# Layer 3 of a decoder kernel: the chosen half of the tokens gathered into 512 slots by one-hot products, and another order of subtractions and maxima in the image attention

## The reference, cut to what matters

```python
scores = (relu(x @ modr_w1 + modr_b1) @ modr_w2 + modr_b2)[..., 0] / TEMP
topk_scores, topk_idx = top_k(scores, k)           # k = 128 of 256
w = softmax(topk_scores, -1)
sorted_idx = sort(topk_idx, -1)
tok = take_along_axis(x, sorted_idx[..., None], axis=1).reshape(B_ * k, D_)
n1 = _ln(tok, ln1_w, ln1_b); uv = n1 @ m_in_w      # 128 -> 2 * 256
u = uv[:, :INNER] * m_conv_w[:, 3] + m_conv_b; res = uv[:, INNER:]
sp = u @ m_xproj_w                                 # 256 -> 33
y = u * (sp[:, 16:32].sum(-1) * sp[:, -1])[:, None] * silu(res)
tok = tok + y @ m_out_w
n2 = _ln(tok, ln2_w, ln2_b)
# gate: the two greatest of softmax(n2 @ moe_r_w + moe_r_b) over 8 experts, normalised
h1 = gelu(einsum('nd,edh->enh', n2, moe_w1) + moe_b1)   # hidden 512
tok = tok + gated sum over e of (h1 @ moe_w2 + moe_b2)
out = x.at[arange(B_)[:, None], sorted_idx].set(tok.reshape(B_, k, D_) * w[..., None])
```

## Time and profile before

| | before |
|---|---|
| runs, us | 4619.43, 4628.18, 4628.18 |
| profiled execution, its own time, us | 4625.78 |
| its span (first to last instruction), us | 4624.1 |
| PE busy | 3545.3 us, 77% |
| DVE busy | 3007.0 us, 65% |
| ACT busy | 1899.2 us, 41% |
| POOL busy | 390.9 us, 8% |
| mean granted TensorE clock | 0.868 |

### The profile page before, as it was taken

How to read it: one execution, slowest core, us unless ns; L and a number is a source line. 1 busy time by engine, 2 the same in 40 slices (tenths; PEclk the granted TensorE clock), 3 DMA queues, 4 the chain that set the end, 5 groups by cost and what they waited for, 6 DMA issues and landing times. The chain is left out here.

```text
span 4624.1 us, 53788 instructions
## 1 busy us (share of the span) xinstructions
PE 3545.3 (77%) x21514; PEld 1886.8 (41%) x21514; DVE 3007.0 (65%) x4129; ACT 1899.2 (41%) x2110; POOL 390.9 (8%) x150
## 2 busy tenths in 40 slices
PE   5699999999999955577777773556654776687569
PEld 3434444444444423233335552423322454454357
DVE  4466666666766676498896446599996455535541
ACT  2255555555555532244442223244442344344223
POOL 0001010100001000000000000044440000001000
PEclk9899999999999977799997896666667888798789
DMA  2000000000000000100002001000000110000000
GB/s 76 9 0 0 1 0 0 0 0 0 0 0 0 1 11 12 20 7 8 8 1 87 28 2 39 1 0 0 0 0 3 36 37 9 37 1 1 0 12 31
DMA packets 12876, 55.75 MB, mean 12 GB/s; under 512 B 2209, under 2 KB 2721, under 8 KB 11970
## 3 DMA queue, kind: packets, MB, share of 16 engines
q1 hardware_dynamic: 12626, 52.31, 3.8%
HBM read 48.50 MB, written 0.52 MB: 11 GB/s over the span
## 5 line engine op out<-in xcount | busy, mean ns | idle before, releaser
L985 PE MATMUL banks<-L0x_q_context,L0x_context 96*128 96x512 f32 (+1 forms) x1632 | 743.5, 597 | 10.8 <-ACT L0x_ring L1054 10.2
L996 PE MATMUL banks<-L0x_ring,L0x_context_rows 128*97 128x512 f32 (+1 forms) x1632 | 737.1, 594 | 1.8 <-ACT L0x_ring L1040 1.8
L1054 ACT COPY L0x_ring<-banks 128x1024 f32<-128x1024 f32 (+1 forms) x416 | 413.0, 995 | 648.4 <-PE banks L985 648.4
L1103 DVE TENSOR_TENSOR L0x_maxima<-L0x_maxima,L0x_ring 128x1024 f32<-128x1024 f32 (+1 forms) x288 | 342.7, 1195 | 261.1 <-ACT L0x_ring L1054 260.1
L1082 DVE TENSOR_TENSOR L0x_ring<-L0x_ring,L0x_greatest 128x2048 f32<-128x2048 f32 (+1 forms) x208 | 458.2, 2205 | 45.9 <-ACT L0x_ring L1054 45.9
L985 PEld LDWEIGHTS banks<-L0x_q_context,L0x_context 96*128 96x128 f32 (+1 forms) x1632 | 302.8, 188 | 415.2 <-issue 393.7
L996 PEld LDWEIGHTS banks<-L0x_ring,L0x_context_rows 128*97 128x97 f32 (+1 forms) x1632 | 263.7, 164 | 433.0 <-issue 429.7
L1040 ACT ACTIVATE L0x_ring<-L0x_ring 128x2048 f32<-128x2048 f32 (+1 forms) x208 | 384.1, 1847 | 8.6 <-DVE L0x_ring L1082 8.6
L1462 ACT ACTIVATE L1x_probs<-banks 128x2048 f32<-128x2048 f32 (+1 forms) x112 | 196.6, 1756 | 263.0 <-PE banks L1392 221.1
L1495 DVE TENSOR_REDUCE L1x_maxima<-banks 128x3 f32<-128x1203 f32 (+1 forms) x176 | 241.6, 1373 | 90.8 <-PE banks L1361 90.8
L1361 PE MATMUL banks<-L1x_k,L1x_q 32*128 32x401 f32 x1024 | 182.1, 593 | 119.7 <-DVE L1x_maxima L1495 104.3
(11 more groups left out here) (918 smaller groups left out, 5439.5 us busy)
## 6 DMA issues: line engine op xcount, KB each, us to landing
L1f_expert_weights<-in_L1f_experts SPq DMA_DIRECT2D x16, 512.0 KB, 9.6
L2f_expert_weights<-in_L2f_experts SPq DMA_DIRECT2D x8, 512.0 KB, 5.6
L3a_expert_weights<-in_L3a_experts SPq DMA_DIRECT2D x8, 512.0 KB, 4.9
L3f_expert_weights<-in_L3f_experts SPq DMA_DIRECT2D x8, 512.0 KB, 6.2
L1x_k<-L1x_k_rows SPq DMA_DIRECT2D x64, 50.0 KB
L0x_context_rows<-in_context_rows SPq DMA_DIRECT2D x1, 2448.0 KB, 29.1
L0x_context<-in_context SPq DMA_DIRECT2D x1, 2401.5 KB, 20.6
L1x_context<-in_context SPq DMA_DIRECT2D x4, 600.4 KB, 5.0
```

The source lines that it names most:

```text
L985: mm = pe.matmul(k.ps[0:height(j), i, :], c1[:, j * P:j * P + height(j)], q1[:, u // 2 % 2, :], start=True, stop=True)
L996: mm = pe.matmul(k.ps[0:CW, bank, :], rows1[0:height(j), j, :], ring[0:height(j), s % RING, i, :], start=s == FIRST[u] and i == 0, stop=s ...
L1054: act.copy(ring[0:r, s % RING, 2 * p:2 * p + len(pair), :], k.ps[0:r, 2 * p:2 * p + len(pair), :]).then_inc(copied, 1)
L1103: dve.tensor_tensor(o, before, ring[0:r, s % RING, 2 * p:2 * p + m, :], ALU.max).then_inc(maxed, 1)
```

## The change

`normalise_columns`, `linear_columns`, `linear_rows`, `one_hot`, `experts`, `gate_bias` and `softmax_experts` get a parameter `tiles` (8 where not given). In `layer3_attention` a chosen token's position plus one (0 for others) is compared with the numbers 1 to 128, which gives a one-hot matrix `into` for each tile. Products of `into` with the rows put the 512 chosen tokens into 4 tiles `picked`, and everything up to the experts runs with `tiles=4`. The transposed one-hots (`back`) put weighted result minus `picked` back to the tokens' places at the end, straight onto the residual; the unchosen rows come in by an addition in the slot stage, and the softmax weights are looked up by slot in one pass. In `attend_image` DVE's order becomes another.

```diff
 def experts(..., tiles=TILES):
+    halves = tiles // 4
...
-                first(0, 0)
-                first(0, 1)
+                for half in range(halves):
+                    first(0, half)
                 for e in range(E):
-                    for half in range(2):
+                    for half in range(halves):
                         second(e, half)
                         if e + 1 < E:
                             first(e + 1, half)
...
 def layer3_attention(k):
...
             @block.tensor
...
                 mm.then_inc(counted, 1)
+                for t in range(TILES):
+                    pe.wait_ge(spread, t + 1)
+                    mm = pe.matmul(k.ps[:, 1, t // TPB * P:(t // TPB + 1) * P], into[:, t, :], z0[:, t, :],
+                                   start=t % TPB == 0, stop=t % TPB == TPB - 1)
+                mm.then_inc(gathered, 1)
+                for t in range(TILES):
+                    mm = pe.transpose(k.ps[:, 2 + t // 4, (t % 4) * P:(t % 4 + 1) * P], into[:, t, :], k.ident[:])
+                mm.then_inc(turned, 1)
             @block.scalar
             def _(act):
+                act.wait_ge(gathered, 1)
+                act.copy(picked[:].rearrange("p b c -> p (b c)"), k.ps[:, 1, :])
                 act.wait_ge(ready, 1)
                 act.activation(sB[:], sB[:], ACT.Exp).then_inc(exped, 1)
+                act.wait_ge(turned, 1)
+                act.copy(back[:].rearrange("p t c -> p (t c)"), k.ps[:, 2:4, :].rearrange("p a n -> p (a n)"))
             @block.vector
...
+                dve.wait_ge(counted, 1)
+                step(dve.scalar_tensor_tensor(out=at[:], in0=k.ps[:, 0, 0:TILES], scalar=1.0, in1=chosen[:], op0=ALU.add, op1=ALU.mult))
+                for t in range(TILES):
+                    dve.tensor_scalar(into[:, t, :], k.count[:], at[:, t:t + 1], None, ALU.is_equal).then_inc(spread, 1)
                 step(dve.tensor_reduce(best[:, 0], s4, X, ALU.max))
                 dve.tensor_tensor(s4, s4, best[:, 0, :, None].broadcast_to(full), ALU.subtract).then_inc(ready, 1)
+                dve.tensor_tensor(k.x[:], k.x[:], z0[:], ALU.add)
                 dve.wait_ge(exped, 1)
                 step(dve.scalar_tensor_tensor(out=sB[:], in0=rB[:], scalar=CAP - 0.5, in1=sB[:], op0=ALU.is_lt, op1=ALU.mult))
                 step(dve.tensor_reduce(best[:, 0], s4, X, ALU.add))
-                step(dve.reciprocal(best[:, 1], best[:, 0]))
-                step(dve.tensor_tensor(s4, s4, best[:, 1, :, None].broadcast_to(full), ALU.mult))
-                dve.wait_ge(counted, 1)
-                step(dve.tensor_copy(at[:], k.ps[:, 0, 0:TILES]))
-                for t in range(TILES):
-                    step(dve.scalar_tensor_tensor(out=tmp[:, 0], in0=r4[:, t // TPB], scalar=at[:, t:t + 1], in1=s4[:, t // TPB],
-                                                  op0=ALU.is_equal, op1=ALU.mult))
-                    step(dve.tensor_reduce(weight[:, t:t + 1], tmp[:, 0], X, ALU.add))
-        normalise_columns(k, z0, k.z, k.zT, column_gain=w["gain"], column_shift=w["shift"])
+                dve.reciprocal(best[:, 1], best[:, 0])
+                step(dve.scalar_tensor_tensor(out=sB[:], in0=rB[:], scalar=slot[:], in1=sB[:], op0=ALU.is_equal, op1=ALU.mult))
+                step(dve.tensor_reduce(weight[:], s4, X, ALU.add))
+                step(dve.tensor_tensor(weight[:], weight[:], best[:, 1], ALU.mult))
+        normalise_columns(k, picked, k.z, k.zT, column_gain=w["gain"], column_shift=w["shift"], tiles=B)
...
-        experts(k, "L3a", ew, k.zT, gates, acc, w["mb1"], ACT.Gelu, ImageLast(k.image_ahead))
+        experts(k, "L3a", ew, k.zT, gates, acc, w["mb1"], ACT.Gelu, ImageLast(k.image_ahead), tiles=B)
...
+            @block.tensor
+            def _(pe):
+                for t in range(TILES):
+                    pe.wait_ge(changed, t // TPB + 1)
+                    pe.matmul(k.ps[:, t // 4, (t % 4) * P:(t % 4 + 1) * P], back[:, t, :], tok[:, t // TPB, :], start=True, stop=True).then_inc(returned, 1)
             @block.vector
             def _(dve):
-                step = Steps(dve, own)
-                full = [P, TILES, P]
-                step(dve.tensor_tensor(tok[:], tok[:], acc[:], ALU.add))
-                step(dve.tensor_tensor(tok[:], tok[:], weight[:, :, None].broadcast_to(full), ALU.mult))
-                step(dve.tensor_tensor(tok[:], tok[:], z0[:], ALU.subtract))
-                step(dve.tensor_tensor(tok[:], tok[:], chosen[:, :, None].broadcast_to(full), ALU.mult))
-                step(dve.tensor_tensor(tok[:], tok[:], z0[:], ALU.add))
-        accumulate(k, tok)
+                dve.tensor_tensor(tok[:], tok[:], acc[:], ALU.add).then_inc(added, 1)
+                dve.wait_ge(added, 1)
+                for b in range(B):
+                    dve.scalar_tensor_tensor(out=tok[:, b, :], in0=tok[:, b, :], scalar=weight[:, b:b + 1], in1=picked[:, b, :],
+                                             op0=ALU.mult, op1=ALU.subtract).then_inc(changed, 1)
+                for half in range(2):
+                    dve.wait_ge(returned, 4 * half + 4)
+                    x = k.x[:, 4 * half:4 * half + 4, :].rearrange("p t c -> p (t c)")
+                    dve.tensor_tensor(x, x, k.ps[:, half, :], ALU.add)
...
 def attend_image(...):
...
-            maximum(0)
+            first_half(0)
+            third(0)
+            fold(0)
+            first_half(1)
             for b in range(B):
+                shift(b, 0)
                 if b + 1 < B:
-                    maximum(b + 1)
-                shift(b)
+                    third(b + 1)
+                shift(b, 1)
+                shift(b, 2)
+                if b + 1 < B:
+                    fold(b + 1)
+                shift(b, 3)
                 if b >= 2:
                     finish(b - 2)
+                if b + 2 < B:
+                    first_half(b + 2)
```

More of the change, by code:

```diff
@@ L220, with normalise_columns @@
 ACT_TILES = (3, 6, 7)
-def normalise_columns(k, src, rows, dstT, gain=None, shift=None, column_gain=None, column_shift=None, eps=1e-5, values=None):
-    shared = ACT_TILES if gain is None else ()
-    mine = [t for t in range(TILES) if t not in shared]
+def normalise_columns(k, src, rows, dstT, gain=None, shift=None, column_gain=None, column_shift=None, eps=1e-5, values=None, tiles=TILES):
+    shared = [t for t in ACT_TILES if t < tiles] if gain is None else ()
+    mine = [t for t in range(tiles) if t not in shared]
+    near = tiles // 2
+    middle = near * P
     with k.stage() as (block, signal):
@@ L237, in _ @@
         def _(pe):
-            for t in range(TILES):
+            for t in range(tiles):
                 if t in shared:
@@ L2045, in first @@
                     for f in range(4):
-                        n = 8 * e + 4 * half + f
+                        n = 4 * halves * e + 4 * half + f
                         if n >= U:
@@ L2406, in _ @@
             def _(dve):
-                for half in range(2):
+                for half in range(tiles // 4):
                     dve.wait_ge(turned, 4 * (half + 1))
@@ L2942, in layer3_attention @@
         with k.stage() as (block, signal):
-            own, counted, ready, exped = signal(), signal(), signal(), signal()
+            own, counted, ready, exped, spread, gathered, turned = (signal() for _ in range(7))
             @block.tensor
```

139 lines of the change are left out of this document (74 added, 65 removed).

## The result

| | before | after |
|---|---|---|
| runs, us | 4619.43 to 4630.65, median 4628.18 | 4522.71 to 4533.09, median 4525.15 |
| profiled execution, us | 4625.78 | 4533.09 |
| its span, us | 4624.1 | 4531.4 |
| mean granted TensorE clock | 0.868 | 0.87 |

The ratio after to before is 0.9783, 95% interval 0.9771 to 0.9795: 2.2% faster, about 103 us. The forecast was 4530 with the range 4510 to 4560.

A forecast was written before the change was run, and what follows sets the result against it. PE bounds layer 3's experts, engine chains its small stages, waits for exponentials the image attentions. Gains 48.8, 20.4, 4.3, 26.6 less 2.2 make 97.9 us: 4625.78 to 4527.9, as median 4530; range 4510 to 4560.

The forecast's parts named there:

- Experts: Layer 3's experts' stage: half the tokens, an added 0.94 us wait per turn; 116.03 to 67.2 us, gain 48.8.
- Small stages: Stages ahead of layer 3's experts, 8 tiles to 4: 63.35 us before, gain 20.4, bounds 14 and 26.
- Slot stage: Layer 3's slot stage, 15.60 us before: DVE waits for the counting products; loss 2.2 us, bounds -1 and +4.
- Last stage: Layer 3's last stage with the accumulation, 8.02 us: fewer, shorter passes at full clock; gain 4.3 us, bound 2.5.
- Attentions: Both image attentions: the new DVE order shortens PE's waits before the first additions; gain 26.6 us together.
- Rival 1: Image attentions gain nothing, as DVE's new head-of-line waits hold back the subtractions; 4557 us, chance 12%.
- Rivals 2 and 3: Short rests lower the clock: in the experts' stage, 4583 us, chance 6%; in experts and both attentions, 4644 us, chance 4%.
- Rival 4: Two-deep weight loading holds up layer 3's experts because turns are half as long; a few us, inside the range.
- A sign of being wrong: Stretches outside the two changed layers would change by more than 2 us.

The follow-up runs named there:

- experiment two units ahead: The changed kernel, with PE's list in the experts' stage running two units ahead (first 0, first 1, second 0, first 2); 4515.60 us, ratio 0.9766.
- slot-order experiment: The changed kernel, with DVE's three passes ahead of the wait for counted positions and ACT's exponential ahead of its copy of the gathered rows; 4523.11 us.
- single bank: The changed kernel, with one PSUM bank instead of three for the hidden products of layer 3's experts and one for the second products; 4571.02 us.
- four with two units ahead: The changed kernel with experts two units ahead, alone (4515.60 us) or with slot and exponential edits (4516.39, repeated 4513.22; exponential earlier still 4508.65 us).
- half changes: Changed kernel with DVE's old order in the image attention, 4557.58 us; kernel before with only the new order, 4598.59 us.

## Why the prediction was right

The forecast of 4530 us was made as 97.9 us of stage gains; 96.7 were measured in the same stages, and no term is off by more than 1 us. That the median came within 5 us of the forecast says less: the difference of the medians is 103.0 us and that of the profiled executions 92.7, so with every stage as it is the whole times could have missed by some 5 us either way.

- **Experts**, 67.2 predicted, 67.87 measured. The added wait is there, eight times, from `first`'s end to `second`'s start 4052.53 - 4048.15 - 3.44 = 0.94 us, as predicted. The missing 0.1 us a turn is in `second`, which takes 3.67 instead of 3.57 when it starts after a rest. The experiment two units ahead shows that this wait was the only one: with it covered the turn is 7.01 us, that of before. Costing the image pieces at nothing held. The stage's start took 6.5 us instead of 6.9, since the clock rose earlier, which offsets a part of the 0.1 us a turn.
- **Small stages**, 43.0 predicted, 42.42 measured, but by parts that partly cancel. Between the first products of the stages, the way from the 33-wide rows to the output rows shrank by 6.1 us (10.74 to 4.68), where 3.4 for the rows and a part of the 2.6 for the rest had been forecast: PE's 33-wide products took 2.17 us instead of half of 6.71, since the clock was high for them. The norm stage gave 2.2 instead of 2.5. In the slot-order experiment the same 33-wide products took 3.60 us. So the term came out right in sum, partly by luck: what the 33-wide products take is 1.4 us apart between these two states of the clock, and the forecast had no reason for either.
- **Slot stage**, 17.8 predicted, 17.95 measured. DVE waited 5.59 us for the counted positions (5.3). A compare took 1.66/8 = 0.21 us (0.27), near the lower bound. The forecast called it a quarter of L2965's work, but 128 columns against 1024 are an eighth, 0.15 us, so the reason given for 0.27 was wrong and its size not far off. ACT's exponential ended 12.6 us into the stage (12.3) and DVE idled 1.95 us for it, as the timetable had it. The reordered stage shows the cause: with the three passes ahead of the wait, and the exponential with them, it takes 12.4 us.
- **Last stage**, 3.7 predicted, 3.92 measured, at clock 1.00 as taken. That could have gone the other way: in five of the experiments (the single bank and the four with two units ahead) the clock fell behind the same rest of 1.84 us, and the products took 0.5 to 0.9 us more.
- **Attentions**, 26.6 predicted, 25.8 measured. The four waits came out at 1.41, 0.35, 1.41 and 1.41 us against 1.4, 0.4, 1.4 to 1.5 and 1.41. The missing 0.8 us are in the clock at the attentions' heads (2.63 and 2.42 us against 2.00); the order alone, in the kernel before, gave 27.0. DVE's new head-of-line wait exists (2.17 us idle before `first_half(3)`, twice the forecast's 1 us), and PE never noticed: the subtraction behind it ended at 4138.26, and ACT began its exponential at 4141.10, behind the copy of the sums.
- **Rival 1** (attentions gain nothing) fell with the first profile and with both half changes. **Rivals 2 and 3** (short rests pull the clock down) were the serious ones, and one chance in ten was perhaps fair at the time, but they fell: the clock is 0.97 in the experts' stage and 0.95 and 0.96 in the attentions. The single-bank experiment has many more rests in the experts than the change, each about as long (0.44 to 0.84 us idle in the trace, 0.78 in the change), and the clock is 1.00. The step from one rest of 1.41 us to "full clock behind it" was weaker than it looked, though: in the eleven profiles with the new order the clock fell behind such a rest in 2 of 22 attentions (last section). The Trainium skill (TensorE: Matmul & The Clock Gate, section "A second HAM failure mode: psum-queue depth-cycling") tells of a kernel whose short rests between groups made the clock go to and fro; in the experts' stage of this case the trace does not agree: 62.33 us of work in 93.84, cut by rests of up to 0.84 us, ran at 2.4 GHz. **Rival 4** (weight loads) fell: no turn begins with a wait for a load, at a DMA share of 0.13 instead of 0.08.
- **A sign of being wrong** was named that did come true: a stretch outside the two layers changed by more than 2 us, namely the 6 us ahead of the slot stage. The code there is the same, and this is scatter: in the repeat of the changed kernel the slot stage began at 3931.51 us, in other kernels with the same code ahead of it anywhere from 3922.79 us on. The sign was set tighter than the scatter.
- **Not predicted**: the 1.6 us ahead of the first attention, of which 1.3 are in the stage that projects the image keys. Its first PE work used to come 9.8 us after PE's last, at 1.2 GHz; now the last stage has PE products, the rest is 1.76 us, and the first units run at 2.4 GHz. It is small, but it is a stage that no edit touched.

The profiled execution of after was the slowest of its four runs. So the sum of the stages fits better than the difference of these two executions, 92.7 us: the other 6 us lie ahead of the slot stage.

## What to carry to other kernels

When a loop over two independent halves is cut to one half, look at what the second half covered: here a gelu's tail of 0.94 us appeared in every turn, and issuing two units ahead instead of two halves removed it. On an in-order engine, place a wait behind the work that doesn't need it; beside that, only such moves paid here, while taking turns for its own sake gave nothing (the first subtraction ahead of the next batch's fold 26 us, three passes ahead of the counted positions 5.6, the exponential ahead of the copy of the sums 3.7 to 5). And where a few us are at stake, compare stages in the traces: with the same code in front of the changed stages, kernels differed by up to 13 us there. A gain in one stage can also be lost in part behind it, through PE's clock: 2.4 of 5.6 us in the slot stage, 1.5 of 8.4 us in the experts.

## What the runs showed of the hardware that was not expected

- **Equal code differs by 13 us through PE's clock.** The code ahead of the slot stage is the same in the changed kernel and in the one two units ahead. The two stretches, from the start of each:

```profile
0.00:3922.79 3922.79, 3033.35 (x17931) 1543.37 (x17935) 2690.79 (x3391) 1657.15 (x1787) 371.43 (x136) 0.87 0.04 12
```

```profile
0.00:3935.85 3935.85, 3046.94 (x17934) 1550.11 (x17935) 2691.83 (x3391) 1657.22 (x1787) 371.49 (x136) 0.87 0.04 12
```

  The first (two units ahead) is 13.1 us shorter, PE is busy for 13.6 us less with the same instructions, ACT for 0.1 and DVE for 1.0. The difference builds up in stretches such as this one, where the same instructions on all engines take 126.0 and 128.8 us, and only PE's busy time and the granted clock (0.92 and 0.88) differ:

```profile
2543.00:2669.00 126.00, 96.30 (x1374) 68.10 (x1372) 55.98 (x120) 34.79 (x44) 3.82 (x2) 0.92 0.07 26
```

```profile
2552.10:2680.90 128.80, 99.02 (x1374) 70.03 (x1372) 55.98 (x120) 34.78 (x44) 3.82 (x2) 0.88 0.07 25
```

  The start of the slot stage differs by 8.3 to 8.5 us also among kernels of one group (3926.45 to 3934.78 us, 3924.18 to 3932.67 us). So most of the scatter of this kernel's time lies in where PE's clock rises and falls; why it rises where it does was not settled.
- **Rests and the clock.** In these traces the length of a rest alone doesn't decide what follows. The experts' rests of up to 0.84 us never cost the clock. Behind the attentions' 1.41 us it was kept nearly always, but fell twice: in the single-bank kernel's first attention (3.32 us instead of 1.94, shown above), and in the second attention of the kernel with the new order alone, where the 16 products of batch 2 took 5.36 us instead of 3.67. Behind the last stage's 1.84 us the products took 2.05 us in six profiles and 2.54 to 2.93 us in five. In the old order's attentions 1.2 GHz followed the rests of 2.68 us and more; but in the changed kernel the 33-wide products came behind a rest of 3.55 us and still ran at a granted clock of 0.86.

```profile
4262.66 5.36 PE L3888 MATMUL banks<-L3x_big,L3x_v 128*65 128x256 f32 x16 [1.41 <-ACT L3x_big L3935]
```
- **POOL's partition maximum and DVE.** In the old order the last three of an attention's maxima took 1.97 us each while DVE had a subtraction at the head of its queue; in the changed kernel 1.16 to 1.17, with DVE idle or on a short step as they began. With all subtractions first it took 2.13 us in the first attention's second batch, where a DVE maximum of 1.22 us began in the same moment, and 1.06 in the two after. It cost nothing here. Spans on POOL are rough, and the cause was not tested by itself.
